# Opening of a one-core perceiver kernel in another order: keys and values of batch 0 ahead of norms and queries, in half transfers

## The chip, the cores and the metric

The kernel runs on one core of one Trainium2 chip. The metric is the time of one execution on the device in microseconds (us); lower is better. Runs of the kernel are compared on the same chip.

## What is computed (the reference, cut)

One layer of a perceiver on x of [16, 64, 512]: cross attention to a context of [16, 1601, 512], self attention with a low-rank addition (LoRA) to its queries and values, and a mixture of 20 experts of which each token takes two. Dropped below: reshapes and the constants.

```python
h = layernorm(x)                                     # 1024 rows of 512
q, k, v = h @ w_q.T, ctx @ w_k.T, ctx @ w_v.T        # 16 heads of 32
s = where(mask == 0, -1e9, q @ k.T / sqrt(32))       # mask [64, 1601], one for all batches
x = x + (softmax(s) @ v) @ w_o.T
x = x + self_attention(layernorm(x))                 # qkv with LoRA on q and v, projection
h = layernorm(x)
g = top2(softmax(gelu(h @ wg1 + bg1) @ wg2 + bg2))   # gates of 20 experts
x = x + sum_e g[:, e] * (h @ We[e] + be[e])
```

## The kernel before, in words

Every product of matrices is made in float32 by three matmuls (`mm3`, L196 to L198): an operand is split into a high part, rounded by ScalarE (ACT, `weight_hi`, `context`, `turn_x`: a copy into the rounded type), and a low part, the rest, subtracted by VectorE (DVE, `weight_lo`, `context`, `turn_x` with `rest`, L1081). So nothing is multiplied before ACT and then DVE have gone over it.

The 1601 keys are held as five chunks of 400, the last chunk first. A cross attention step n handles one batch: four products give its 400 keys for all heads (`k_part`, 12 matmuls of 400 columns each), three or four give tiles of 128 values (`v_part`, 12 matmuls of 512 columns), `s_part` gives scores in two halves, DVE takes their maxima under the mask (`maxima`), ACT the exponentials (`exps`), GpSimd (POOL) divides by the sums, DVE transposes (`turn`), 16 small transfers on the SP queue shuffle blocks between partitions (`shuffle`), and `pv_part` multiplies with the values one step later. Segment 0 has 16 steps, one for each batch. Further segments would follow only where the mask needs more than the first chunk: `cm`, `rows`, `fl`, `fr`, `frow` and `used` (L1103) work that out into `ids`, and `count` is read by every engine with `value_load` ahead of step 0.

Each engine runs its own instructions in order, and semaphores hold them back. `wait_ge(S["v_w"], 2)` means that the engine stops until the second weight's low part is done. The lists `uses` and `at` give each product one of three PSUM banks in turn.

The opening before: the SP queue loads constants, the first half of x, the mask twice (64 partitions each), then w_q, context 0, w_k, the second half of x, mask and exclusions, and w_v when w_q's buffer is free. DVE takes means and variances of x (`bn`), reduces the mask (L1292), scales by it (L1294 to L1301, L1118) and normalizes (`apply_x`). TensorE transposes x by fours (`turn_x`, `turn4`, L202), makes the first half of the queries, the rest of the transposes and the four key products of batch 0, and then the second half of the queries, where L198 ends at 60.6 us. Step 0 makes its scores and values after that.

Step 1 has extra work: after the last value evictions ACT rounds the output weight (`out_weight_hi`), DVE subtracts (`out_weight_lo`), and only then come `turn(1, 5)` to `turn(1, 7)`, which `shuffle(1)` and so `pv_part(1, ...)` of step 2 wait for.

At the experts: `tok` (L1585) names which rows of x each block of 128 tokens takes. POOL gathers them from memory (`load_tokens`, L1745), TensorE transposes (`turn_tokens`), and each `block_of` is one block. Between the table's product (L669) and the first transposes stand the expert biases: eight products of the gates with `be` (L659), which DVE adds to `x_sb` (L1590). When all blocks are done, rows are read back and added (L1632), and x is stored.

## Time and profile before

| | |
|---|---|
| median of 3 runs | 717.66 us (716.87 to 718.05) |
| profiled execution | 719.19 us, its span 717.4 us |
| TensorE (PE) busy in the span | 647.0 us (90%) |
| VectorE (DVE) busy | 444.9 us (62%) |
| ScalarE (ACT) busy | 324.6 us (45%) |
| GpSimd (POOL) busy | 286.7 us (40%) |
| data moved | 108.26 MB, mean 151 GB/s |

The span runs from the first to the last instruction that the profiler shows, and the execution's own time is 1.8 us longer. The busy shares are means over stages with different limits, so a change in the opening is read from the opening's rows.

### The profile page before, as it was taken

The page shows a single profiled execution, that of the slowest core. Times are in us where ns is not written, and L with a number is a line of the kernel's source. Part 1 is how long each engine was busy: PE and PEld are TensorE (multiplying, and loading weights), DVE is VectorE, ACT ScalarE, POOL GpSimd, SP SyncE. Part 2 cuts the span into 40 slices and gives each one's busy share as a digit, 9 for nine tenths or more (in the row PEclk, how much of TensorE's full clock was granted, in tenths as well). Part 3 has the DMA queues.
Part 4 walks back from the last instruction along what each step waited for, and adds up shares of the span by engine and source line. Part 5 has one row for each costly group of instructions (what it writes and reads, how often), then busy time and mean ns, then how long its engine had stood idle before and what let it go on. Part 6 is the DMA issues. An engine that isn't in the chain of part 4 may idle for free.

```text
span 717.4 us, 15912 instructions
## 1 busy us (share of the span) xinstructions
PE 647.0 (90%) x6305; PEld 529.0 (74%) x6305; DVE 444.9 (62%) x1002; ACT 324.6 (45%) x601; POOL 286.7 (40%) x259
## 2 busy tenths in 40 slices
PE   0899998999999999999999979999999748999960
PEld 0697887788888788888788868877787535888850
DVE  4855574755665645765654556445575467899956
ACT  1425453444434444544443335334365430899940
POOL 0003535544445534355534234321243315787420
PEclk9999999999999999999999999999999965999995
DMA  8511535566554566455556540210011933999819
GB/s 282 194 60 47 118 99 142 136 165 164 115 127 125 128 164 138 116 129 130 146 120 159 126 150 1 74 60 3 2 60 63 382 114 125 383 401 396 291 53 347
DMA packets 42695, 108.26 MB, mean 151 GB/s; under 512 B 8164, under 2 KB 8548, under 8 KB 41714
## 3 DMA queue, kind: packets, MB, share of 16 engines
q1 hardware_dynamic: 38210, 98.73, 46.6%
q0 software_dynamic: 4400, 8.41, 3.2%
q8 instruction: 53, 0.87, 0.5%
q14 instruction: 32, 0.26, 0.1%
HBM read 66.13 MB, written 13.44 MB: 111 GB/s over the span
## 4 chain that ended last, share of the span: by engine, by line
PE 79%; DVE 6%; PEld 3%; DMA 3%; issue 3%; ACT 2%; SPq 2%; POOL 0%; PEldq 0%; POOLq 0%; ACTq 0%; DVEq 0%
PE bank L196 23%; PE bank L198 21%; PE bank L197 21%; PE bank L337 4%; PE bank L321 3%; PE bank L202 3%; DMA raw<-in_wq 2%; SPq L1819 1%; DVE x_sb L1632 1%; PE bank L558 1%; PEld bank L198 1%; PE bank L545 1%; DMA wr<-scratch_ys 1%; PEld bank L196 1%; PE bank L659 1%
## 5 line engine op out<-in xcount | busy, mean ns | idle before, releaser
L1658 POOL TENSOR_SCALAR pp<-pp,rl 128x400 f32<-128x400 f32 x128 | 162.9, 1290 | 176.7 <-DVE rl L1163 176.7
L815 ACT ACTIVATE pp<-pp,acc 128x400 f32<-128x400 f32 x128 | 79.0, 619 | 68.0 <-DVE acc L1222 68.0
L1222 DVE CUSTOM_DVE_ANT_0 pp<-bank,cap 128x400 f32<-128x400 f32 x128 | 65.9, 571 | 61.1 <-PE bank L321 61.1
L1212 DVE STREAM_TRANSPOSE raw<-pp 128x512 f32<-128x512 f32 x128 | 83.9, 690 | 10.4 <-POOL pp L1658 5.8
L196 PE MATMUL bank<-chi,wk 128*128 128x400 f32 x256 | 90.1, 352 | 0.0
L197 PE MATMUL bank<-clo,wk 128*128 128x400 f32 x256 | 88.3, 345 | 0.0
L198 PE MATMUL bank<-chi,wk 128*128 128x400 f32 x256 | 88.3, 345 | 0.0
L196 PE MATMUL bank<-wv,chi 128*128 128x512 f32 x200 | 82.2, 411 | 0.0
L197 PE MATMUL bank<-wv,chi 128*128 128x512 f32 x200 | 78.7, 393 | 0.0
L198 PE MATMUL bank<-wv,clo 128*128 128x512 f32 x200 | 78.4, 392 | 0.0
L196 PE MATMUL bank<-wh,xu 128*128 128x512 f32 x148 | 63.4, 428 | 4.2 <-POOL xu L1684 3.5
L198 PE MATMUL bank<-wh,xu 128*128 128x512 f32 x148 | 59.8, 404 | 0.0
L197 PE MATMUL bank<-wh,xu 128*128 128x512 f32 x148 | 59.4, 402 | 0.0
L755 ACT ACTIVATE vv<-bank 128x512 f32<-128x512 f32 x50 | 28.1, 597 | 63.1 <-PE bank L198 32.7
L196 PEld LDWEIGHTS bank<-chi,wk 128*128 128x128 f32 x256 | 48.0, 188 | 10.0 <-issue 9.4
L1150 DVE COPY kk<-bank 128x400 f32<-128x400 f32 x32 | 18.3, 573 | 58.0 <-PE bank L198 58.0
L196 PEld LDWEIGHTS bank<-wv,chi 128*128 128x128 f32 x200 | 37.6, 188 | 18.7 <-issue 10.8
L197 PEld LDWEIGHTS bank<-clo,wk 128*128 128x128 f32 x256 | 48.1, 188 | 0.6
L198 PEld LDWEIGHTS bank<-chi,wk 128*128 128x128 f32 x256 | 48.0, 188 | 0.0
L198 PEld LDWEIGHTS bank<-wv,clo 128*128 128x128 f32 x200 | 37.7, 189 | 8.6
L755 ACT ACTIVATE kk<-bank 128x400 f32<-128x400 f32 x32 | 16.1, 504 | 61.1 <-PE bank L198 61.1
L197 PEld LDWEIGHTS bank<-wv,chi 128*128 128x128 f32 x200 | 37.8, 189 | 6.5
(241 smaller groups left out, 1296.8 us busy)
## 6 DMA issues: line engine op xcount, KB each, us to landing
pt<-raw SPq DMA_DIRECT2D x256, 128.0 KB, 2.4
wr<-in_We SPq DMA_DIRECT2D x13, 1024.0 KB, 11.1
craw<-in_ctx SPq DMA_DIRECT2D x16, 800.0 KB, 4.7
raw<-in_We SPq DMA_DIRECT2D x8, 1024.0 KB, 10.8
acc<-in_We SPq DMA_DIRECT2D x6, 1024.0 KB, 11.7
scratch_xn<-acc SPq DMA_DIRECT2D x16, 256.0 KB
wr<-scratch_ys SPq DMA_DIRECT2D x8, 512.0 KB, 7.1
x_sb<-in_x SPq DMA_DIRECT2D x2, 1024.0 KB, 9.0
```

The source lines that it names most:

```text
L196: pe.matmul(o, lhs[0], rhs[0], start=start, stop=False)
L197: pe.matmul(o, lhs[0], rhs[1], start=False, stop=False)
L198: return pe.matmul(o, lhs[1], rhs[0], start=False, stop=stop)
L202: last = pe.transpose(bank[0:n, k * 128:(k + 1) * 128], of(k), ident)
L321: last = pe.matmul(scores[64 * c:64 * c + 64, j, :], qc[r, 2 * half + c, 64 * b:64 * b + 64], kk[r, 2 * half + c, :], start=True, stop=True)
L337: last = pe.matmul(turned[32 * j:32 * j + 32, g, :].rearrange("p (a q) -> p a q", a=2), vv[:, (25 * (n // 8) + 3 * (n % 8) + i4) % 4, 128 ...
L755: return act.activation(dst, src, ACT.Copy)
L815: act.activation(frame(p8), frame(p8), ACT.Exp, bias=bias, scale=-1.0, accum_out=total).then_inc(S["a_exp"], 1)
L1150: dve.tensor_copy(kk[:, g, :], at("k", 4 * n + g)[:, 0:CW]).then_inc(S["v_k"], 1)
L1212: dve.transpose(square[:, :, :, 32 * p8:32 * p8 + 32].rearrange("p o i x -> p i o x"), pp[:, c:c + 512].rearrange("p (i o x) -> p i o x", ...
L1222: dve.tensor_tensor_reduce(out=frame(p8), in0=scores[:, p8 % 4, :], in1=cap[:, :], scale=-1.0, scalar=nm[:, b, p8:p8 + 1] if seg else 3e38 ...
L1658: pool.tensor_scalar(frame(p8), frame(p8), rl[:, n % 2, p8:p8 + 1], None, ALU.mult).then_inc(S["g_pn"], 1)
```

## The change

The first four transfers become halves of w_k and of context 0, each half of 128 partitions. Constants and `lora` follow, then w_v (when the first half of w_k has landed), half of x, the mask once over 128 partitions, w_q into free space of `acc` (when the second half of w_k has landed), and the other half of x. TensorE begins with the keys of batch 0 (`first_keys`): the first two of the four blocks of 128 inputs for all four groups, then the other two, in banks 4 to 7. Two value tiles follow, then the sums over masks (`any_masked`, a new product that brings together the two halves of the mask), the transposes of x and a third value tile, and four query products with the small products of the mask's bookkeeping and of LoRA between them. The first scores of step 0 come ahead of the second half of the queries. The low parts of w_v and w_q are split: DVE takes blocks 2 and 3, POOL blocks 0 and 1. `used` moves from the opening to step 1 behind `out_weight_lo`; the `value_load`s move to step 3. `pp` no longer shares its place with `xt`, so the maxima don't wait for the last query (`p_q` 8) any more; `shuffle(0)` does now, as `pt` still shares it. POOL's clearing of `pp` moves to the start. At the experts, biases 3 to 7 on TensorE and all eight additions on DVE move behind the last block. Some small tiles move into `zero`, `acc`, `raw` and `pp`, and the counts in waits change with the order.

```diff
+        pp = sb("pp", [128, 8 * D + PW], f32, lasting)
...
+        lora = acc[0:16, 0:D].rearrange("p (j n) -> p j n", j=4)
+        wq_in = acc[:, 2048:4096].rearrange("p (k n) -> p k n", k=4)
...
+        uses = [("v", 0), ("v", 1), ("x", 0), ("x", 1), ("v", 2), ("x", 2), ("x", 3)] + [("q", m) for m in range(4)]
+        uses += [("x", 4), ("x", 5), ("v", 3), ("x", 6), ("x", 7)] + [("q", 4 + m) for m in range(4)]
...
+            def any_masked():
+
+                pe.wait_ge(S["d_cst"], 16)
+                pe.wait_ge(S["v_cap"], 1)
+                for c in range(2):
+                    for h in range(2):
+                        last = pe.matmul(pb[3][64 * c:64 * c + 64, 0:NC_], ident[:, 64 * h:64 * h + 64], cm, start=(h == 0),
+                                         stop=(h == 1))
+                last.then_inc(S["p_ids"], 1)
...
+            def first_keys():
+
+                c = columns(0)
+                for half in range(2):
+                    pe.wait_ge(S["v_w"], half + 1)
+                    pe.wait_ge(S["v_ctx"], half + 1)
+                    for g in range(4):
+                        for k in (2 * half, 2 * half + 1):
+                            last = mm3(pe, at("k", g)[:, 0:CW], [w[:, k, g * 128:(g + 1) * 128] for w in wk],
+                                       [chi[:, k, c], clo[:, k, c]], k == 0, k == 3)
+                        if half:
+                            last.then_inc(S["p_k"], 1)
 
...
+            def opening():
+                first_keys()
+                v_part(0, 0)
+                v_part(0, 1)
+                any_masked()
+                turn_x(0)
+                turn_x(1)
+                v_part(0, 2)
+                turn_x(2)
+                turn_x(3)
+                queries(0)
+                turn_rows()
+                queries(1)
+                count_chunks()
+                queries(2)
+                lora_products()
+                queries(3)
+                s_part(0, 0)
+                turn_x(4)
+                turn_x(5)
+                v_part(0, 3)
+                turn_x(6)
+                turn_x(7)
+                s_part(0, 1)
+                for m in range(4, 8):
+                    queries(m)
...
-            biases(range(3, 8))
             turn_tokens(0)
...
+            biases(range(3, 8))
...
+            def first_half(half, w_arrived, ctx_arrived):
+                ks = slice(2 * half, 2 * half + 2)
+                act.wait_ge(*w_arrived)
+                copy(wk[0][:, ks], raw[:, 1, ks]).then_inc(S["a_w"], 1)
+                act.wait_ge(*ctx_arrived)
+                copy(chi[:, ks, columns(0)], craw[:, ks]).then_inc(S["a_ctx"], 1)
...
+            def opening():
+                first_half(0, (d_raw[0], 16), (S["d_ctx"], 16))
+                first_half(1, (d_raw[1], 16), (S["d_k1"], 16))
+                weight_hi(wv, raw[:, 0], (d_raw[0], 32))
+                k_part(0, 0)
+                k_part(0, 2)
+                value(0, 0)
+                weight_hi(wh[0], wq_in, (d_raw[1], 32))
+                value(0, 1)
+                turn_x(0)
+                turn_x(1)
+                value(0, 2)
+                turn_x(2)
+                turn_x(3)
+                queries(0)
+                context(1)
+                for m in range(1, 4):
+                    queries(m)
+                turn_x(4)
+                turn_x(5)
+                value(0, 3)
+                turn_x(6)
+                turn_x(7)
+                exps(0, 0, 0)
+                exps(0, 0, 1)
+                queries(4)
+                exps(0, 0, 2)
+                queries(5)
+                exps(0, 0, 3)
+                queries(6)
+                queries(7)
...
             def weight_lo(dst, src, n):
                 dve.wait_ge(S["a_w"], n)
-                rest(dst[1][:, :, :], src, dst[0][:, :, :]).then_inc(S["v_w"], 1)
+                rest(dst[1][:, 2:4, :], src[:, 2:4], dst[0][:, 2:4, :]).then_inc(S["v_w"], 1)
+
+            def first_half(half):
+                ks = slice(2 * half, 2 * half + 2)
+                dve.wait_ge(S["a_w"], half + 1)
+                rest(wk[1][:, ks], raw[:, 1, ks], wk[0][:, ks]).then_inc(S["v_w"], 1)
+                dve.wait_ge(S["a_ctx"], half + 1)
+                rest(clo[:, ks, columns(0)], craw[:, ks], chi[:, ks, columns(0)]).then_inc(S["v_ctx"], 1)
...
-                    if n == 0:
-                        dve.wait_ge(S["p_q"], 8)
...
+            def row_scales():
+
+                dve.wait_ge(S["p_ids"], 1)
+                own.on(dve.tensor_scalar(cm, pb[3][:, 0:NC_], 0.0, None, ALU.not_equal))
+                dve.wait_ge(own.sem, own.n)
+                own.on(dve.tensor_reduce(rows[:, 0:1], cm, AX.X, ALU.max))
+                dve.wait_ge(own.sem, own.n)
+                dve.tensor_scalar(rows[:, 1:2], rows[:, 0:1], SCALE, None, ALU.mult)
+                own.on(dve.tensor_scalar(rows[:, 2:3], rows[:, 0:1], -1.0, 1.0, ALU.mult, ALU.add))
+                dve.wait_ge(own.sem, own.n)
+                dve.tensor_scalar(fl[:, 1:NC_], cm[:, 1:NC_], rows[:, 2:3], None, ALU.max).then_inc(S["v_ids"], 1)
...
+            def opening():
+                dve.memset(fl[:, 0:1], 1.0)
+                first_half(0)
+                first_half(1)
+                weight_lo(wv, raw[:, 0], 3)
+                dve.wait_ge(d_x[0], 16)
+                for i in range(4):
+                    own.on(bn(i))
+                variance(0, 4)
+                dve.wait_ge(S["d_par"], 32)
+                dve.tensor_reduce(cm, mska, AX.X, ALU.max, apply_absolute_value=True).then_inc(S["v_cap"], 1)
+                k_part(0, 1)
+                k_part(0, 3)
+                row_scales()
+                scaled(0, 4)
+                apply_x(0)
+                apply_x(1)
+                weight_lo(wh[0], wq_in, 4)
+                turn_x(0)
+                apply_x(2)
+                turn_x(1)
+                apply_x(3)
+                turn_x(2)
+                turn_x(3)
+                dve.wait_ge(d_x[1], 16)
+                for i in range(4, 8):
+                    own.on(bn(i))
+                variance(4, 4)
+                dve.wait_ge(S["p_ids"], 2)
+                dve.tensor_reduce(fr, pb[3][0:NC_, 0:128], AX.X, ALU.max).then_inc(S["v_ids"], 1)
+                context(1)
+                dve.wait_ge(S["p_ids"], 3)
+                dve.tensor_copy(frow[:, 0:10], pb[3][0:1, 0:10]).then_inc(S["v_ids"], 1)
+                scaled(4, 4)
+                apply_x(4)
+                apply_x(5)
+                make_cap(0)
+                lora_folds()
+                turn_x(4)
+                apply_x(6)
+                turn_x(5)
+                apply_x(7)
+                maxima(0, 0, 0)
+                turn_x(6)
+                turn_x(7)
+                maxima(0, 0, 1)
+
...
                         out_weight_lo()
+                        used()
+                    elif n == 3:
+                        dve.wait_ge(S["v_ids"], 5)
+                        counted.append(dve.value_load(ids[0:1, 5:6], min_val=1, max_val=5))
...
-            biases(range(8))
...
+            biases(range(8))
...
+            pool.memset(one32[:, :], 1.0)
+            alone(pool.memset(pp[:, 0:8 * D].rearrange("p (t c) -> p t c", t=8)[:, :, 0:PW], 0.0))
+            alone(pool.memset(pp[:, 8 * D:8 * D + PW], 0.0))
+
+            def weight_lo(dst, src, n):
+                pool.wait_ge(S["a_w"], n)
+                pool.tensor_tensor(dst[1][:, 0:2, :], src[:, 0:2], dst[0][:, 0:2, :].bitcast(f32),
+                                   ALU.subtract).then_inc(S["g_w"], 1)
...
+            weight_lo(wv, raw[:, 0], 3)
             power(0, 4, (S["v_var"], 1), S["g_rstd"])
+            weight_lo(wh[0], wq_in, 4)
             power(4, 4, (S["v_var"], 2), S["g_rstd"])
-            pool.wait_ge(S["p_q"], 8)
-            alone(pool.memset(pp[:, 0:8 * D].rearrange("p (t c) -> p t c", t=8)[:, :, 0:PW], 0.0))
-            alone(pool.memset(pp[:, 8 * D:8 * D + PW], 0.0))
-            pool.wait_ge(S["v_ids"], 5)
...
+            sp.dma_start(raw[:, 1, 0:2], t["wk"][:, 0:2]).then_inc(d_raw[0], 16)
+            sp.dma_start(craw[:, 0:2, :], t["ctx"][0, 0][:, 0:2]).then_inc(S["d_ctx"], 16)
+            sp.dma_start(raw[:, 1, 2:4], t["wk"][:, 2:4]).then_inc(d_raw[1], 16)
+            sp.dma_start(craw[:, 2:4, :], t["ctx"][0, 0][:, 2:4]).then_inc(S["d_k1"], 16)
             sp.dma_start(cst[:, :], t["cst"]).then_inc(S["d_cst"], 16)
             sp.dma_start(lora[:, :, :], t["lora"]).then_inc(S["d_par"], 16)
-            xv = t["x"].rearrange("(i b) q d -> i (b q) d", b=2)
+            sp.wait_ge(d_raw[0], 16)
+            sp.dma_start(raw[:, 0], t["wv"]).then_inc(d_raw[0], 16)
             sp.dma_start(x_sb[:, 0:4, :], xv[0:4].rearrange("i p d -> p i d")).then_inc(d_x[0], 16)
-            for h in range(2):
-                sp.dma_start(mska[64 * h:64 * h + 64, :, :], t["rows"]).then_inc(S["d_cap"], 16)
-            sp.wait_ge(S["d_cst"], 16)
-            sp.dma_start(raw[:, 0], t["wq"]).then_inc(d_raw[0], 16)
-            sp.wait_ge(d_x[0], 16)
-            sp.dma_start(craw[:, :, :], t["ctx"][0, 0]).then_inc(S["d_ctx"], 16)
-            sp.wait_ge(S["d_cap"], 32)
-            sp.dma_start(raw[:, 1], t["wk"]).then_inc(d_raw[1], 16)
+            sp.dma_start(mska, t["rows"]).then_inc(S["d_par"], 16)
+            sp.wait_ge(d_raw[1], 16)
+            sp.dma_start(wq_in, t["wq"]).then_inc(d_raw[1], 16)
             sp.dma_start(x_sb[:, 4:8, :], xv[4:8].rearrange("i p d -> p i d")).then_inc(d_x[1], 16)
 
             def chunk_of(seg):
                 return sp.value_load(ids[0:1, seg:seg + 1], min_val=0, max_val=4)
...
                 if n:
                     sp.wait_ge(S["p_pv"], 2 * n)
+                else:
+                    sp.wait_ge(S["p_q"], 8)
```

## Rows read from the trace of the kernel before

**Rows 1.** Busy time by stage: PE, PEld, DVE, ACT, POOL, granted clock, DMA, GB/s

```profile
200.00:300.00 100.00, 100.00 (x1167) 83.62 (x1166) 59.34 (x148) 44.81 (x106) 46.13 (x37) 1.00 0.51 125
```

**Rows 2.** Chain of waits in the opening: start us, us, what

```profile
3.40 12.49 DMA raw<-in_wq
...
25.32 0.72 PE bank L196
26.05 0.43 PE bank L197
...
30.50 0.23 PE bank L196
...
38.90 0.87 PE bank L202 x8
```

**Rows 3.** Timeline of PE: the first key product of step 1

```profile
73.77 0.34 PE L196 MATMUL bank<-chi,wk 128*128 128x400 f32 x1
```

**Rows 4.** Busy time by half microseconds at the start (columns as rows 1)

```profile
3.50:4.00 0.50, 0.00 (x0) 0.00 (x0) 0.00 (x0) 0.00 (x0) 0.00 (x0) 1.00 0.50 78
...
4.50:5.00 0.50, 0.00 (x0) 0.00 (x0) 0.00 (x0) 0.00 (x0) 0.00 (x0) 1.00 1.07 418
```

**Rows 5.** Groups of instructions by shape: busy us, mean ns | idle before

```profile
L755 ACT ACTIVATE xt<-bank 128x512 fp32r<-128x512 f32 x8 | 4.6, 597 | 6.2 <-PE bank L202 6.2
...
L755 ACT ACTIVATE wh<-raw 128x2048 fp32r<-128x2048 f32 x1 | 1.9, 1912 | 13.9 <-DMA raw<-in_wq 13.9
...
L1222 DVE CUSTOM_DVE_ANT_0 pp<-bank,cap 128x400 f32<-128x400 f32 x16 | 8.2, 571 | 15.0 <-PE bank L321 15.0
...
L1081 DVE TENSOR_TENSOR xt<-bank,xt 128x512 fp32r<-128x512 f32 x8 | 5.4, 682 | 1.6 <-ACT xt L755 1.6
...
L1081 DVE TENSOR_TENSOR wh<-raw,wh 128x2048 fp32r<-128x2048 f32 x1 | 2.3, 2293 | 0.1
...
L1721 POOL TENSOR_TENSOR wh<-raw,wh 128x512 fp32r<-128x512 f32 x4 | 5.1, 1294 | 0.0
```

**Rows 6.** Timeline of DVE in the opening: mask scaling (first, last), `used` (first, last)

```profile
15.71 0.17 DVE L1294 TENSOR_SCALAR cm<-cm 128x5 f32<-128x5 f32 x1
...
16.50 0.23 DVE L1118 TENSOR_SCALAR rstd<-rstd,rows 128x4 f32<-128x4 f32 x1
...
29.72 0.14 DVE L1105 TENSOR_TENSOR frow<-frow,cst 1x5 f32<-1x5 f32 x1
...
30.95 0.13 DVE L1113 CAST ids<-frow 1x1 int32<-1x1 f32 x1
```

**Rows 7.** Chain of waits through steps 1 and 2

```profile
95.84 1.92 ACT wh L755
...
114.82 3.16 PE bank L337 x128
```

**Rows 8.** Waits of PE from 100 to 420 us: total, times, longest

```profile
PE bank L337 <- DMA pt<-raw: 2.5, 1, 2.5
```

**Rows 9.** Busy time around that wait (columns as rows 1)

```profile
115.50:116.00 0.50, 0.50 (x32) 0.50 (x25) 0.50 (x3) 0.00 (x0) 0.00 (x0) 0.50 0.97 397
...
118.50:119.00 0.50, 0.50 (x3) 0.44 (x2) 0.50 (x1) 0.50 (x2) 0.50 (x2) 0.68 0.00 0
```

**Rows 10.** Chain of waits ahead of the first expert block

```profile
597.89 5.52 PE bank L659 x10
603.41 1.06 PE bank L202 x4
...
605.96 0.76 PE bank L196
```

**Rows 11.** Tile xi (gathered tokens): gathers, and time to landing

```profile
L1745 POOL DMA_INDIRECT xi<-scratch_xn,tok x15: 997/1026/1541, 598.2 to 624.7; - x15
...
DMA to landing us min/median/max: 2.7/6.2/7.2
```

**Rows 12.** Timeline of DVE at the end: the first additions of expert rows

```profile
701.24 2.99 DVE L1632 SCALAR_TENSOR_TENSOR x_sb<-wr,gmg,x_sb 128x512 f32<-128x512 f32 x4 [8.75 <-DMA wr<-scratch_ys]
```

More of the change, by code:

```diff
@@ new lines, in turn_rows, with count_chunks, lora_products @@
+            def turn_rows():
+                pe.wait_ge(S["v_ids"], 1)
+                pe.transpose(pb[3][0:NC_, 0:128], fl[:, 0:NC_], ident).then_inc(S["p_ids"], 1)
+            def count_chunks():
+                pe.wait_ge(S["v_ids"], 2)
+                pe.matmul(pb[3][0:1, 0:10], fr, cst[0:NC_, 128:138], start=True, stop=True).then_inc(S["p_ids"], 1)
+            def lora_products():
+                pe.wait_ge(S["d_par"], 32)
+                pe.wait_ge(S["v_ids"], 3)
+                for j in range(2):
+                    last = pe.matmul(pb[3][:, j * 128:(j + 1) * 128], lora[:, 2 * j, :], lora[:, 2 * j + 1, :], start=True,
+                                     stop=True)
+                last.then_inc(S["p_ids"], 1)
@@ new lines, in turn_x, with queries @@
+                turn4(pe, at("x", i), lambda k: xn[:, i % 2, k * 128:(k + 1) * 128]).then_inc(S["p_xt"], 1)
+            def queries(m):
+                pe.wait_ge(S["v_w"], 4)
+                pe.wait_ge(S["g_w"], 2)
+                pe.wait_ge(S["v_xt"], m // 4 * 4 + 4)
+                for ready in freed("q", m):
+                    pe.wait_ge(*ready)
+                for k in range(4):
+                    last = mm3(pe, at("q", m)[:, :], [w[:, k, m % 4 * 128:(m % 4 + 1) * 128] for w in wh[0]],
+                               [v[:, k, :] for v in xt], k == 0, k == 3)
+                last.then_inc(S["p_q"], 1)
@@ L784, in k_part, with queries @@
                 copy(kk[:, g, :], at("k", 4 * n + g)[:, 0:CW]).then_inc(S["a_k"], 1)
[L786 to L789 removed]
+            def queries(m):
+                act.wait_ge(S["p_q"], m + 1)
+                copy(qc[:, m % 4, m // 4 * 512:(m // 4 + 1) * 512], at("q", m)[:, :]).then_inc(S["a_q"], 1)
             def early_hi(i):
@@ L820, in exps @@
                                    ACT.Exp).then_inc(S["a_cor"], 1)
+            def opening():
[29 more added lines that the diff above has]
+                queries(7)
             def cross(seg):
-                for n in range(16 * seg, 16 * seg + NB):
+                if not seg:
+                    opening()
+                for n in range(16 * seg or 1, 16 * seg + NB):
                     values = list(range(made(n), made(n + 1)))
@@ L1235, in cross @@
                     make_cap(seg)
+                else:
+                    opening()
                 for n in range(first, last + 1):
@@ L1242, in cross @@
                         k_part(n, 1)
-                    if n < last and n:
-                        context(n + 1)
-                    maxima(n, seg, 0)
-                    maxima(n, seg, 1)
-                    if n == 0:
-                        context(1)
+                        if n < last:
+                            context(n + 1)
+                        maxima(n, seg, 0)
+                        maxima(n, seg, 1)
                     share(n, 0, seg)
@@ L1816, in shuffle @@
                     sp.wait_ge(S["p_pv"], 2 * n)
+                else:
+                    sp.wait_ge(S["p_q"], 8)
                 for a in range(4):
@@ L2024 @@
         "mask": mask.reshape(64, NC, CW)[:, ::-1].transpose(1, 0, 2),
-        "rows": mask.reshape(64, NC, CW)[:, ::-1],
+        "rows": mask.reshape(64, NC, 2, CW // 2)[:, ::-1].transpose(2, 0, 1, 3).reshape(128, NC, CW // 2),
         "excl": excl,
```

249 lines of the change are left out of this document (71 added, 178 removed).

## The prediction

> **What bounds the kernel now.** First the busy time by stage: in the middle of the cross attention TensorE is busy for all of 100 us [rows 1], so there each microsecond by which step 1 begins earlier reaches the end, unless a later wait takes it back. Then the chain of waits through the opening: until 15.9 us it is the transfer of w_q, 12.5 us from its issue; then rounding, low parts, norms and transposes, and TensorE's first query product starts at 25.3 [rows 2]. From there TensorE has no gap until step 1 begins with its first key product at 73.77 [rows 3]. So the opening costs 25.3 us of an almost idle TensorE and 48.45 us of work. Third, the chain through steps 1 and 2: it leaves TensorE for ACT's output weight at 95.84 and returns with the values' product of step 1 at 114.8 [rows 7]; TensorE waited 2.5 us for that shuffle [rows 8]. Fourth, the chain ahead of the experts: biases, then transposes, then block 0 at 605.96 [rows 10].
>
> **Start of TensorE after.** First I estimate the landings. Up to 4.0 us little flows (78 GB/s in the half microsecond before it), and at 4.5 the rate is 418 GB/s [rows 4]; I put 0.3 MB at 4.0 and go on with 380 GB/s. The first half of w_k (0.52 MB) is there at 4.65, that of the context (0.41 MB) at 5.65, the second halves at 7.0 and 8.1. ACT takes 0.60 us for 512 columns and 1.91 for 2048, DVE 0.68 and 2.29, POOL 1.29 for 512 [rows 5]. Between these, 1024 columns are 1.04 on ACT and 1.22 on DVE, 800 columns 0.85 and 0.98. The halves pass: ACT w_k 4.7 to 5.7, DVE its low part to 7.0 while ACT rounds the context, DVE the context's low part to 7.9. TensorE starts at 8.0. Bounds: 7.0 if data come a microsecond sooner, 9.2 if the four pieces share the rate and the first land only at about 6.
>
> **Work from there to step 1.** The same products as before in another order: 48.45 us from 25.32 to 73.77, four transposes of which lie ahead of 25.3 now and come after the start: 1.75 (0.87 for eight single ones [rows 2] is 0.44 for each four). Small products (masks, rows, counts, LoRA) I put at 1.5, between nothing and the 2 us that several isolated ones would be. Cold matmuls: 0.43 us at first and 0.23 later in the old opening [rows 2], that is the level of 1.2 and then of 2.4 GHz for 512 columns, and the new opening pays a similar stretch on keys, so no difference.
>
> New gaps on TensorE, each a chain through other engines:
> - Before transpose 0: `any_masked` comes after value tile 1, so DVE's scaling can begin only then: 15.71 to 16.73 in the old order [rows 6], 1.0 us, then one norm of 512 columns (no more than the low part's 0.68) and hand-overs: 1.8.
> - Before query 0: the last two transposed tiles pass ACT (0.5 and 0.6) and DVE (0.68), less the 0.44 in which the last transposes run, with value tile 2's eviction ahead: 1.65.
> - Before the first scores: the last query's eviction on ACT, 0.60 and hand-overs: 0.7.
> - Before the second scores: value tile 3 and two x tiles on ACT (0.5, 0.5, 0.6), the last low part on DVE (0.68), two maxima (0.57 each), less 0.9 of transposes: 2.7.
>
> Together 6.85. Step 1 begins at 8.0 + 48.45 + 1.75 + 1.5 + 6.85 = 66.55.
>
> What hides the rest: w_v's low part on POOL is 2.6 us (twice 1.29) from about 14.0 and is wanted at 18.9, after 10.9 us of keys; alone on DVE it would be 2.3. w_q's on POOL runs 24.2 to 26.8 and is wanted at 32.9. Were that cover gone, query 0 would wait for POOL one for one. x's norms and the mask's reduction (half as many columns) end before 21 on DVE, some 4 us ahead of `any_masked`. `make_cap` and LoRA's folds lie under queries. POOL's clearing of `pp` moves to where POOL has nothing. On the SP queue, w_v waits for w_k's first half and w_q for its second; nothing in front of them is late for them, and w_q has until 22 on ACT. `shuffle(0)` now waits for `p_q` 8, that is until step 1 begins, where 16 steps of it and its landing fit under the 16 us of TensorE work before it is read. The reads of `count` fall on step 3 for all engines; I cost them at nothing, since TensorE's stood between queries and scores before, in the stretch without gaps, and at most at some tenths.
>
> **The clock.** After the 2.5 us wait [rows 8] the granted clock was 0.50 in 115.5 to 116 and came back at about 118.7 (0.68 in 118.5 to 119) [rows 9]; the values' product took 3.16 us there [rows 7]. About 3.5 us at half rate lose 1.75. Of the new gaps the one of 2.7 us is longer than that wait, so I charge it 1.75; those of 1.8 and 1.65 are shorter and I charge them nothing; the bounds are 0 and 1.75 for each. The Trainium skill, "TensorE: Matmul & The Clock Gate", section "HAM oscillation — how this bites in real kernels", says that a kernel whose TensorE waits between bursts falls back to the half clock and pays for the warm-up each time. The row on the 2.5 us wait agrees; for shorter gaps no row here shows it, and if the rule held for all three the sum would be 3.5 us more.
>
> So step 1 begins at 68.3 and the opening gains 73.77 - 68.3 = 5.5 us.
>
> **What is given back.** `used` stood at 29.72 to 31.08 [rows 6] in a stretch of DVE that nobody waited for. It now follows `out_weight_lo` in step 1, in front of the transposes 5 to 7 that `shuffle(1)` waits for, and that chain ends in the wait of 2.5 us [rows 7, 8]. That chain starts from TensorE's own third value tile, so it moves with TensorE and the wait doesn't shrink by the earlier start: it grows by 1.36. Loss 1.4; none if something else on that chain gave way.
>
> **Experts.** `tok` releases the gathers; the first is issued at 598.2 and a gather lands 2.7 us from issue at the least [rows 11], so at 601.0 or later. TensorE was with the biases until 603.41 [rows 10]. Without them: transposes 0 end at about 602.1 (1.06), ACT and DVE 0.60 and 0.68 [rows 5], while transposes 1 wait for the second gather, 1.3 us behind the first, and block 0 can start at 603.6 to 605.0. I take 604.2, a gain of 1.8 (1.0 to 2.3). The biases cost nothing at the end: DVE is free there for 8.75 us until 701.24 [rows 12], eight additions are some 5 us, and five products at the 5.52 us of now [rows 10] fit as well.
>
> **Sum.** -5.5 + 1.4 - 1.8 = -5.9. On the profiled execution, 719.19 to 713.3; its time is 1.5 above the median of 717.66, so for the median 711.8. No change within 0.2% (1.4 us) can be told from none.
>
> **Rivals.**
> 1. The forecast, 711.8: chance 0.50 (its own range 710.3 to 713.3).
> 2. The clock stays up through the 2.7 us gap. 1.75 less: 710.0. With an early start (7.0) and 2.3 at the experts, 708.5. Chance 0.22.
> 3. The clock falls at all three gaps: twice 1.75 more, 715.3. For it speaks the one wait that did so [rows 8, 9], against it that the gaps are a third shorter. Chance 0.15. This is the case in which the Trainium skill's section named above holds throughout.
> 4. The gain is lost further on: the wait at step 2 grows by more than `used` because `shuffle(0)` behind `p_q` 8 delays the queue, or the experts don't start earlier. It needs 4.5 us more; same as before, 716.5 to 718.5. Against it: TensorE is busy throughout behind step 2 [rows 1]. Chance 0.08.
> 5. Slower: the halves do not land first. All transfers are issued in a row and may share the engines, as w_q, issued at 3.4, needed 12.5 us [rows 2]. If w_k and the context landed like that, at about 13 to 15, TensorE would start at 15 to 16, and beyond 13.9 (8.0 + 5.9) the change loses: 719 to 720. Against it: the four are first in the queue, and w_q had 2 MB ahead of it. Chance 0.05.
>
> The range is 708.3 to 715.7: it leaves out rivals 4 and 5 and the far ends of 2 and 3. Faster 0.87, same 0.08, slower 0.05.
>
> **What would show it.** First key matmul at 8.0 (7.0 to 9.2); first key product of step 1 at 68.3; four gaps of 1.8, 1.65, 0.7 and 2.7 us on TensorE with a granted clock of 0.5 after the last alone; a wait of 3.9 us for the shuffle in step 2; block 0's start 1.8 us nearer to `tok`; additions of biases ended before the first expert rows. Wrong would be made most easily by the landing times and by the clock.

## The result, and the profile after

| | before | after |
|---|---|---|
| median, us | 718.62 (716.87 to 720.73, 6 executions) | 712.25 (710.65 to 713.12, 5 executions) |
| ratio, 95% interval | | 0.9907 [0.9882, 0.9932] |
| profiled execution, us | 719.19, span 717.4 | 712.70, span 710.8 |
| mean granted clock | 0.959 | 0.959 |

The forecast was 711.8 us, range 708.3 to 715.7, a gain of 5.9; the medians differ by 6.4. Two disturbed executions, one of 761 us here and one of 1073 us in the first experiment, are left out. The total is right, but three of its terms were not; so first the path through the changed kernel, stretch by stretch, on the two profiled executions.

The waits of TensorE in the first 200 us of the changed kernel (total, times, longest):

```profile
PE bank L193 <- DVE clo L1147: 8.3, 1, 8.3
PE bank L354 <- DVE acc L1297: 2.7, 1, 2.7
PE bank L199 <- DVE raw L1176: 2.6, 1, 2.6
PE bank L372 <- DMA pt<-raw: 2.4, 1, 2.4
PE bank L193 <- DVE xt L1147: 1.8, 1, 1.8
PE bank L354 <- issue: 1.8, 1, 1.8
PE bank L354 <- ACT qc L796: 0.8, 1, 0.8
```

TensorE starts at 8.3 (forecast 8.0); the four gaps of the opening are 2.6, 1.8, 0.8 and 2.7 (forecast 1.8, 1.65, 0.7, 2.7). The wait for the second shuffle is 2.4 us, as in [rows 8] and not 3.9 as forecast, but a new wait of 1.8 us stands at L354, before the first scores of step 2. The first key product of step 1, in the timeline of PE:

```profile
69.32 0.35 PE L193 MATMUL bank<-chi,wk 128*128 128x400 f32 x1
```

That is 4.45 us earlier than in [rows 3]; 5.5 were forecast. The values' products of steps 0, 1 and 2, in the chains of waits, of the changed kernel and then of the kernel before (where the middle one is in [rows 7]):

```profile
85.97 1.92 PE bank L372 x128
...
111.55 1.99 PE bank L372 x128
...
132.87 1.92 PE bank L372 x128
```

```profile
90.41 1.95 PE bank L337 x128
...
137.70 1.92 PE bank L337 x128
```

From the first to the third of them it is 46.90 us after and 47.29 before, so the stretch as a whole is not longer, though 1.4 us were forecast for `used`. Its two parts differ, though: from the first to the second it is 25.58 us for 24.41, 1.17 longer, and from the second to the third 21.32 for 22.88, since in the kernel before the clock fell at the second one ([rows 9]) and here it did not. The timeline of DVE in step 1 shows where it stands (first `used` instruction, then the key eviction behind it):

```profile
95.53 0.14 DVE L1180 TENSOR_TENSOR zero<-zero,cst 1x5 f32<-1x5 f32 x1
...
98.63 0.52 DVE L1225 COPY kk<-bank 128x400 f32<-128x400 f32 x1
```

The eviction ends at 99.15 and the scores start at 99.26. The 1.8 us wait, which the view puts down to "issue", is thus one for DVE.

The experts: the release of the row numbers, the start of block 0, and the end (the loads of result rows by SP, and DVE's last additions), and then the release and the end in the kernel before:

```profile
591.07 0.18 DVE tok L1672
...
598.47 0.76 PE bank L193
```

```profile
690.06 3.99 SPq L2050 DMA_DIRECT2D wr<-scratch_ys  x8
```

```profile
704.00 2.99 DVE L1718 SCALAR_TENSOR_TENSOR x_sb<-wr,gmg,x_sb 128x512 f32<-128x512 f32 x4 [0.61 <-DMA wr<-scratch_ys]
```

```profile
597.07 0.18 DVE tok L1585
```

```profile
697.97 4.47 SPq L1953 DMA_DIRECT2D wr<-scratch_ys  x8
```

```profile
704.90 8.79 DVE L1632 SCALAR_TENSOR_TENSOR x_sb<-wr,gmg,x_sb 128x512 f32<-128x512 f32 x12 [0.67 <-DMA wr<-scratch_ys]
```

From release to block 0 it is 7.40 us (8.89 before, 605.96 of [rows 10] less 597.07), from release to the first load of results 98.99 (100.90 before). From that load to the end of the last addition it is 16.93 us (15.72 before, 697.97 to 713.69).

The sum over the two executions: opening -4.45, steps 1 and 2 -0.39, from there to the release of the row numbers -1.17, experts -1.91, end +1.21, the rest +0.1; together -6.6, the difference of the spans. The opening gave less than forecast, the delay by `used` was made up by a fall of the clock that did not come, the experts gave what was forecast, and two terms that the sum did not have nearly cancel.

### The profile page after: what moved, and what is told of

Its sections match the earlier page's. It is cut to its first block, busy times and chain, and to the rows that moved or that the text cites. A ratio compares the mean times of both kernels' runs of the same rounds, so it can differ in the third digit from the quotient of the medians.

```text
span 710.8 us, 15960 instructions
## 1 busy us (share of the span) xinstructions
PE 642.0 (90%) x6313; PEld 525.4 (74%) x6313; DVE 442.3 (62%) x1004; ACT 325.2 (46%) x603; POOL 294.2 (41%) x261
## 4 chain that ended last, share of the span: by engine, by line
PE 80%; DVE 5%; issue 4%; PEld 3%; DMA 3%; ACT 2%; SPq 2%; POOL 0%; DVEq 0%; PEldq 0%; POOLq 0%; ACTq 0%
PE bank L193 23%; PE bank L195 21%; PE bank L194 21%; PE bank L372 4%; PE bank L354 4%; PE bank L199 3%; DMA wr<-scratch_ys 2%; SPq L1917 1%; PE bank L599 1%; PE bank L586 1%; PEld bank L195 1%; PEld bank L193 1%; PEld bank L194 1%; DMA craw<-in_ctx 1%; PE bank L615 1%
## 5 line engine op out<-in xcount | busy, mean ns | idle before, releaser
L193 PEld LDWEIGHTS bank<-wv,chi 128*128 128x128 f32 x200 | 38.0, 190 | 17.5 <-issue 9.4
L1147 DVE TENSOR_TENSOR xu<-bank,xu 128x512 fp32r<-128x512 f32 x44 | 29.8, 684 | 24.9 <-ACT xu L796 18.5
L796 ACT ACTIVATE kk<-bank 128x400 f32<-128x400 f32 x32 | 16.1, 504 | 60.9 <-PE bank L195 60.9
```

The lines of the kernel that those rows point to most:

```text
L193: pe.matmul(o, lhs[0], rhs[0], start=start, stop=False)
L796: return act.activation(dst, src, ACT.Copy)
L1147: return dve.tensor_tensor(dst, src, hi.bitcast(f32), ALU.subtract)
```

## The experiments

All medians stand beside the kernel before on the same chip: 718.61 us in experiments 1 to 4, 718.55 in 5's first execution and in 6 to 8, and on another chip 719.01 in the timed part of 5 and in 9 to 11. The changed kernel itself came again first, as a reference.

**1. The changed kernel, unaltered.**

> The changed kernel unaltered, once more, for its spread and as the reference of the other runs of this call. Theory: time 712 us (710.5 to 713.2), ratio to the kernel before 0.991; the idle times of TensorE in the opening come again as 2.6, 1.8, 0.8 and 2.7 us, because the order of the instructions sets them. Theory A for the clock: the order sets its falls too, so the granted clock is 0.5 at 29 to 31 us and 1.0 after the wait for the second shuffle, as in the first trace. Rival B: the falls depend on the moment, so the places change from one execution to the next with the same gaps, and the time with them by 1.2 to 1.6 us each.

713.12 us, ratio 0.9919 [0.9895, 0.9943]. The gaps are the same four: 2.6, 1.8, 0.8 and 2.7. The falls of the clock are not at the same places. The granted clock of the stretches 28 to 32, 56 to 60 and 100 to 105 us, first in the profiled execution of the result, then in this one (columns as rows 1, the third number from the right is the clock):

```profile
28.00:32.00 4.00, 4.00 (x13) 3.19 (x12) 2.81 (x5) 1.01 (x2) 0.00 (x0) 0.57 0.01 4
56.00:60.00 4.00, 2.85 (x25) 1.89 (x26) 3.12 (x14) 1.73 (x6) 2.82 (x3) 1.00 0.01 4
100.00:105.00 5.00, 5.00 (x32) 4.38 (x24) 3.94 (x12) 2.56 (x8) 1.62 (x2) 1.00 0.76 169
```

```profile
28.00:32.00 4.00, 4.00 (x26) 3.40 (x24) 3.05 (x5) 1.72 (x4) 0.00 (x0) 1.00 0.00 0
56.00:60.00 4.00, 4.00 (x24) 2.58 (x19) 2.85 (x10) 0.57 (x2) 4.00 (x4) 0.57 0.01 4
100.00:105.00 5.00, 5.00 (x31) 4.51 (x17) 4.15 (x12) 2.56 (x8) 1.41 (x2) 0.66 0.81 182
```

Behind the 2.6 us gap TensorE was slowed in one and not in the other; behind the 2.7 us gap it is the reverse; behind the 1.8 us wait of step 2 only the second one fell. Theory A falls, rival B holds for the places. One fall has the same price each time: one minus the clock, summed over the stretch, is 1.7 us (4 times 0.43, 5 times 0.34). So the falls in the column of the granted clock can be listed for every profiled execution of this study (summed in windows of 1 us, 3.4 where two follow each other; the slow first products of TensorE are not in that column):

| execution | falls in the opening, us | falls in steps 1 and 2 |
|---|---|---|
| before | none | 115-119 |
| changed, first | 28-32 | none |
| 1 | 56-60 | 100-105 |
| 2 | 54-59 | 99-103 |
| 3 | 26-34 (3.4) | 112-116 |
| 4 | 56-60 | 100-105 |
| 5, first | 27-31, 58-62 | 112-120 (3.4) |
| 5, timed | 56-60 | 100-105 |
| 6 | 29-33, 60-64 | 104-108 |
| 7 | 28-33 | none |
| 8 | 32-36, 55-60 | none |
| 9 | 31-36 | none |
| 10 | 54-59 | none |
| 11 | 56-61 | 111-115 |

The new opening has one or two falls in each of these, the old one had none.

**2. The mask's product ahead of value tile 1.**

```
                 v_part(0, 0)
+                any_masked()
                 v_part(0, 1)
-                any_masked()
```

> The mask's small product stands ahead of value tile 1 instead of behind it. Theory: the 2.6 us gap ahead of the first transposes is due to that place alone, so it goes (0 to 0.4 us left), DVE's small operation on the zero tile falls from 1.06 to 0.2 us since it no longer meets POOL's low part, and the fall of the clock behind the gap goes too: 2.4 us less in gaps and 1.2 to 1.7 less in slow products, step 1 begins 3.5 to 4 us earlier, time 708.3 to 709. Rival B: the clock falls at the gap of 2.7 us instead, then step 1 begins 2.4 us earlier and the time is 709.8. Rival C: the transposes wait for something else (the norms' reciprocal roots on POOL, the second half of x), the gap stays over 1.5 us and the time over 711.

710.76 us, ratio 0.9889 [0.9867, 0.9912], 2.4 us under experiment 1 by the medians (the intervals overlap). The 2.6 us gap is gone from the waits and DVE's operation took 0.23; one fall of the clock stayed, behind the 2.7 us gap. That is rival B; step 1's first scores came at 74.48 instead of 76.30, 1.8 of its 2.4 us. In this execution TensorE started 0.25 us earlier, but its slow first products lasted 6.3 us instead of 4.2, which at nearly half the rate costs about 0.9.

**3. `used` back in the opening.**

```
                 dve.tensor_copy(frow[:, 0:10], pb[3][0:1, 0:10]).then_inc(S["v_ids"], 1)
+                dve.wait_ge(S["v_ids"], 3)
+                used()
...
                         out_weight_lo()
-                        used()
```

> The seven small operations that work out the list of used chunks go back into the opening, behind the copy of the counts, instead of following the output weight's low part in step 1. Theory: they cost 1.3 us in step 1, by delaying DVE's key eviction, so that the first scores of step 2 wait 0.5 instead of 1.8 us, while the wait for the second shuffle stays at 2.4 to 2.5; nothing is lost in the opening; time 1.3 us less, 710.9. Rival B, as the prediction had it: they lengthen the wait for the second shuffle, which falls to 1.1 us, and the scores still wait 1.8; the same 1.3. Rival C: with 0.5 and 2.5 us of waits, as in the kernel before, the clock falls behind the second one and takes 1.6 us back: time 712.3 or a little more, no gain.

713.00 us, ratio 0.9916 [0.9895, 0.9936]: no gain. The scores of step 2 wait 0.5 us and the shuffle 2.7, and the clock falls behind the shuffle (values' product 3.59 us). Rival C holds in the trace; the medians alone, whose intervals are 2.9 and 3.4 us wide, could not tell 1.3 us from none. The values' products of steps 0, 1 and 2 here:

```profile
87.73 1.92 PE bank L372 x128
...
112.31 3.59 PE bank L372 x128
...
135.24 1.93 PE bank L372 x128
```

From the first to the third it is 47.51 us, against 46.90 and 46.67 with `used` in step 1 (the changed kernel's first execution and experiment 1). But from the first to the second it is 24.58, against 25.58 and 25.31: the delay by `used` is there, and what hides it is the place of the fall.

**4. The experts' biases back in their old place**, the last five products on TensorE as here, the additions on DVE in the same way.

```
             last.then_inc(S["p_tab"], 1)
+            biases(range(3, 8))
             turn_tokens(0)
...
-            biases(range(3, 8))
```

> The experts' biases go back to their old place ahead of the first transposes of the experts. Theory: the experts' first transposes of block 1 begin 2.0 us later against the release of the row numbers (11.8 us, 13.7 in the kernel before), and the tail behind the last block stays as it is in the changed kernel (16.9 us from the first load of results to the last addition), time 2.0 us more: 714.2. Rival B: the additions at the end cause the longer tail (15.7 us in the kernel before), so it shortens by 1.2 us with them gone and the net loss is 0.7: 713. Rival C: nothing at all, because the transfers of the experts' weights set the pace: 712.2.

715.97 us, ratio 0.9961 [0.9943, 0.9979], 2.9 above experiment 1. From release to the first load of results 101.4 us (99.3 in experiment 1, 100.90 before), so 2.1 of it is where the theory has it; from that load to the last addition 16.1. That tail is 15.7 and 16.1 with the biases early and 15.6 to 17.4 in the twelve profiled executions with the biases last; whether they have a part in it is left open.

**5. GpSimd's part of w_q later**, so that it does not meet DVE's scaling, in one execution and then timed.

```
+            pool.wait_ge(S["v_xn"], 2)
             weight_lo(wh[0], wq_in, 4)
```

> GpSimd's share of w_q's low part waits until DVE has written the first two norms, nothing else is altered. Theory: the 0.8 us by which the first gap was longer than forecast (2.6 for 1.8) come from DVE's small operation that took 1.06 us while GpSimd's low part ran; with the two apart it takes 0.2 and the gap is 1.8 us. GpSimd's part still ends before query 0 needs it, so that gap stays at 1.8. Rival: the operation is slow for a reason of its own (its operands, the clearing ahead of it), still takes 1.0, and the gap stays at 2.6.

> GpSimd's share of w_q's low part behind the first two norms once more, now timed, because its only execution so far took 718.75 us: the first gap was 1.8 us, as expected, but the records have falls of the clock that cost 10.2 us ahead of the experts' part, against 5.1 in the changed kernel. Theory: the falls come by chance and do not belong to this edit; the gap of 0.8 us less is all, median 711.5 to 713, some executions up to 718. Rival: the shorter gap brings the falls of the clock with it, and the median is 716 or more.

The first execution took 718.75 us, the five timed ones 713.28 (712.16 to 714.65), ratio 0.9933 [0.992, 0.9946]. In both the first gap is 1.8 us, as forecast for the changed kernel, and the operation takes 0.23. The theory on the gap holds, but it is worth no time that can be measured here. The first execution had four falls more up to 570 us than the changed kernel's first one (12.0 us against 5.1; the 10.2 of the expectation leaves one out), which is more than the 6.1 us between them; that such falls do not belong to the edit is read from the timed executions, none of which came near it. In both executions another operation of DVE met GpSimd's part instead. First the changed kernel, GpSimd then DVE, then the timed one:

```profile
14.38 3.40 POOL L1736 TENSOR_TENSOR wv<-raw,wv 128x1024 fp32r<-128x1024 f32 x1 [12.47 <-ACT wv L796]
...
24.02 2.35 POOL L1736 TENSOR_TENSOR wh<-acc,wh 128x1024 fp32r<-128x1024 f32 x1 [4.01 <-ACT wh L796]
```

```profile
14.26 1.23 DVE L1147 TENSOR_TENSOR wv<-raw,wv 128x1024 fp32r<-128x1024 f32 x1 [3.15 <-ACT wv L796]
...
25.34 1.06 DVE L1316 TENSOR_SCALAR zero<-zero 128x4 f32<-128x4 f32 x1
```

```profile
26.72 3.31 POOL L1736 TENSOR_TENSOR wh<-acc,wh 128x1024 fp32r<-128x1024 f32 x1 [6.25 <-DVE raw L1176]
```

```profile
28.29 2.03 DVE L1176 TENSOR_SCALAR raw<-x_sb,mv,rstd 128x512 f32<-128x512 f32 x1
```

In the changed kernel the operation at L1316 ends at 26.40, GpSimd at 26.37. In the timed one the norm, 0.54 us elsewhere, ends at 30.32, GpSimd at 30.03. And where DVE's low part runs first, GpSimd's takes 3.40 instead of 2.35: 15.49, the end of DVE's, plus 2.35 is 17.84, and it ends at 17.78. So of these operations the one that comes second waits until the first has ended. Other operations of DVE ran beside GpSimd's part unhindered (last section).

**6. Whole transfers of w_k and the context.**

```
-            sp.dma_start(raw[:, 1, 0:2], t["wk"][:, 0:2]).then_inc(d_raw[0], 16)
-            sp.dma_start(craw[:, 0:2, :], t["ctx"][0, 0][:, 0:2]).then_inc(S["d_ctx"], 16)
-            sp.dma_start(raw[:, 1, 2:4], t["wk"][:, 2:4]).then_inc(d_raw[1], 16)
-            sp.dma_start(craw[:, 2:4, :], t["ctx"][0, 0][:, 2:4]).then_inc(S["d_k1"], 16)
+            sp.dma_start(raw[:, 1], t["wk"]).then_inc(d_raw[0], 16)
+            sp.dma_start(craw[:, :, :], t["ctx"][0, 0]).then_inc(S["d_ctx"], 16)
```

> w_k and the context of batch 0 come in one transfer each instead of two halves; the rounding stays in halves. Theory: the start of TensorE follows from the landing of the context's first part, 6.2 us now; with 1.9 MB in two transfers of 1.05 and 0.82 MB, w_k lands at about 7, the context at about 9, and TensorE starts at 10.5 to 11 instead of 8.1; but the second halves are then rounded right away, so the keys of the second half no longer wait and some tenths come back: step 1 begins 2 us later, time 714.5 to 715. Rival: the pieces share the rate from the start, so the last byte of the first halves lands no earlier than the whole would, and TensorE starts at 8 to 9 with the time unchanged.

715.32 us, ratio 0.9955 [0.9939, 0.9972], 2.2 above experiment 1. TensorE starts at 9.6 instead of 8.1, not at 10.5: ACT's first pieces begin at 5.62 and 7.60, at 4.30 and 6.05 in experiment 1. So the start lies between theory and rival, and the time is near the theory's. The halves are worth 1.5 us at the start in this pair; with halves the start lies at 7.5 to 8.6 in twelve traces. With the edit w_v also waits for the whole of w_k, and w_q no longer waits for its second half. 1.7 more of this execution is a second fall of the clock.

**7. The output weight's low part later**, in halves at the ends of steps 2 and 4 instead of step 1.

```
                     if n == 1:
-                        out_weight_lo()
                         used()
+                    if n in (2, 4):
+                        out_weight_lo(n // 2 - 1)
```

> The output weight's low part, which DVE makes at the end of step 1, is made in two halves at the end of steps 2 and 4; the list of used chunks stays in step 1. Theory: DVE's wait for ACT's high part and the 2.3 us of the low part are what delays the turns, the key eviction and the second shuffle, so the 1.8 us wait for the scores and the 0.6 to 2.4 us wait for the shuffle in step 2 both go; a half of 1.2 us fits in the slack of a step (3.0 us, since step 1 was late by 3.0 us after a delay of 6.0). Pulling 3.3 to 4.2 us out of TensorE's idle time also takes away the fall of the clock there; time 708 to 709. Rival B: another transfer or engine ends last right behind, and waits of over 1.5 us appear in steps 2 to 5: 711 or more. Rival C: half of it shows, 710, because the fall of the clock only moves to a later place.

710.15 us, ratio 0.9884 [0.9865, 0.9903]. All waits of TensorE from the start to 200 us:

```profile
PE bank L193 <- DVE clo L1147: 8.6, 1, 8.6
PE bank L354 <- DVE acc L1298: 2.7, 1, 2.7
PE bank L199 <- DVE raw L1177: 2.6, 1, 2.6
PE bank L193 <- DVE xt L1147: 1.8, 1, 1.8
PE bank L354 <- ACT qc L796: 0.8, 1, 0.8
```

```profile
86.37 1.92 PE bank L372 x128
...
107.63 1.93 PE bank L372 x128
...
128.87 1.93 PE bank L372 x128
```

Both waits of step 2 are gone, and so is the fall of the clock there; from the first of the products to the third it is 42.50 us instead of 46.90. The profiled execution took 708.26 us as the theory says; the median, 3.0 us under experiment 1, shows about two thirds of it and lies where rival C has it. The five times lie at 708.3, 708.5 and three at 710.2; a fall of the clock more would be just that distance, but the three were not profiled, so whether it is rival C's later fall stays open.

**8. Experiments 2, 3 and 7 together.**

> The mask's small product ahead of value tile 1, the list of used chunks back in the opening, and the output weight's low part in halves at the end of steps 2 and 4, together. Theory: the gains add up where they are idle time of TensorE: 2.4 us from the first gap and 3.3 to 4.2 us from step 2, with one fall of the clock (1.7 us) left in the opening: time 706 to 707. Rival: the falls of the clock come back at other places and the sum is no better than the best single part, 708.5 or more.

705.66 us (703.70 to 706.28), ratio 0.9823 [0.9802, 0.9844]. The gains add up as the theory has it: 7.5 us under experiment 1, 2.4 from the gap and 4.4 from step 2 being 6.8. By the medians of experiments 2, 3 and 7 alone it would be 5.5; with intervals of some 3 us each the difference cannot be told from none. Two falls in the opening, none in steps 1 and 2.

**9. As 8, with the four maxima of the first scores ahead of the last two low parts of x.**

```
                 maxima(0, 0, 0)
+                maxima(0, 0, 1)
                 turn_x(6)
                 turn_x(7)
-                maxima(0, 0, 1)
```

> As the run with all three, and also DVE takes all four maxima of the first scores ahead of the last two low parts of x. Theory: the second scores wait for the last maximum alone, which now comes 1.2 us earlier and does not wait for ACT; the gap of 2.7 us falls to 0.8 to 1.0, query 4 then waits some 0.3 us for x, so 1.5 to 1.7 us are gained, and the fall of the clock that followed this gap in some executions is rarer: 703.5 to 704.2. Rival: the gap moves in full to query 4, which waits for the last low part as the scores did, and the time stays at 705.7.

704.50 us (703.14 to 705.15), ratio 0.9802 [0.9789, 0.9814], the best of this study. Its waits in the same stretch:

```profile
PE bank L193 <- DVE clo L1147: 7.5, 1, 7.5
PE bank L193 <- DVE xt L1147: 2.3, 2, 1.8
PE bank L354 <- DVE acc L1298: 0.9, 1, 0.9
PE bank L354 <- ACT qc L796: 0.8, 1, 0.8
```

The 2.7 us gap is 0.9, and query 4 waits 0.5: 1.3 us gained in the gaps, 1.2 in the medians (the intervals against the kernel before overlap).

**10. Experiments 2 and 7 without 3**, that is with `used` in step 1.

> The mask's product first and the output weight's low part later, but the list of used chunks stays in step 1. Theory: what it costs (1.3 us of DVE in step 1) only shows as long as step 1 has no slack; with the low part gone from there it fits, and the time is that of all three, 705.5 to 706. Rival: it costs its 1.3 us wherever step 1 ends in the shuffle: 707.

705.52 us (703.65 to 707.44), ratio 0.981 [0.9795, 0.9826], the same as 8. TensorE waits 0.3 us in step 2. With the low part gone from there, `used` costs nothing in step 1.

**11. Both low parts on DVE alone**, GpSimd's calls and TensorE's waits for them left away.

```
-                rest(dst[1][:, 2:4, :], src[:, 2:4], dst[0][:, 2:4, :]).then_inc(S["v_w"], 1)
+                rest(dst[1][:, :, :], src, dst[0][:, :, :]).then_inc(S["v_w"], 1)
```

> The changed kernel with both low parts whole on DVE, nothing on GpSimd. Theory: GpSimd's share is worth nothing, since DVE stands idle ahead of the mask's product (3.8 us) and query 0 waits for x and not for w_q; without it DVE's small operation takes 0.2 us, the first gap is 1.8 us and the time 0.8 us less or the same: 711.5 to 712.5. Rival B: the low part of w_q, 2.3 us on DVE instead of 1.2, delays the low parts of x, query 0 waits about 1.1 us longer: 713.5. Rival C: the low part of w_v comes after TensorE wants it, value tile 0 waits: over 714.

713.39 us (710.11 to 716.34), ratio 0.9918 [0.9894, 0.9942], the same as experiment 1. The operation takes 0.23 us, the first gap is 1.8, query 0 waits 1.5 and not longer. GpSimd's share is worth nothing that this measures.

This trace also settles what `used` costs. It has `used` in step 1 behind the low part, and the clock falls behind the shuffle, as in the kernel before and in experiment 3:

```profile
85.59 1.92 PE bank L370 x128
...
111.48 3.59 PE bank L370 x128
...
134.39 1.51 PE bank L370 x97
```

From the first to the third it is 48.80 us, against 47.29 and 47.51 without `used` there and the fall at the same place: 1.3 to 1.5 us.

## Why the prediction came out right

**Start of TensorE: right**, 8.3 for 8.0 (7.0 to 9.2), and the four pieces do land first. The path was another: the forecast had DVE held by w_k's low part until 7.0; it ended at 6.55, and what set the start was the context's first half, landed at 6.24 instead of 5.65, and the two passes over it. Halves against whole transfers are worth 1.5 us there (experiment 6).

**Work to step 1: right in sum.** 51.7 us were forecast for products old and new; 69.32 less the start, the gaps (7.9) and one fall (1.7) leaves 51.4. Some of that is luck: the slow first products were put as long as before, but lasted 3.3 us in this execution and 4.9 before, which is worth about 0.7, and in the other traces of the new order they lasted 3.3 to 6.5.

**Gaps: one term mis-sized.** "1.8" before transpose 0 measured 2.6. It was worked out from the old order of the small operations, in which GpSimd was idle; the new order put GpSimd's low part beside them, and one of them waited for its end (experiment 5: 1.8 with the two apart). The other three are within 0.15. The gaps together are 7.9 for 6.85, the start is 0.3 late, the work 0.3 less: step 1 was forecast at 68.3 and began at 69.3. The Trainium skill, "SBUF — State Buffer", section "Who interferes with whom", says that VectorE and GpSimd share a pair of ports, and that where a VectorE instruction of certain kinds needs it, the one that issues first holds it for the whole instruction and the other waits. The ends in experiment 5 agree with it.

**The clock: right in size, not in place.** 1.75 was charged for one fall, and a fall costs 1.7. It was charged to the 2.7 us gap because that is the longest. In the first profiled execution the clock fell behind the 2.6 us gap, in experiment 1 behind the 2.7 us one, with the same gaps in both; in experiment 5's first execution and in 8 and 9 it fell behind gaps of 1.8. The length of a single gap does not decide. What the forecast had as three cases with one answer each (one fall, none, three) is a spread from execution to execution, one or two falls here. Nor did the count grow over the whole path: up to 570 us the first profiled execution has three falls and so has the kernel before, which has none in the opening and one in step 2. Of what the prediction cites from the Trainium skill, the traces bear out that a fall is paid for where no wait follows it, and not that each of these gaps brings one; the waits in that section's example are 3 to 5 us, longer than any gap here.

**What is given back: the step that failed.** "it grows by 1.36. Loss 1.4". The wait for the shuffle did not grow, and the stretch did not get longer. The delay itself came: from the values' product of step 0 to that of step 1 it is 25.3 to 26.4 us in the eight traces that have `used` behind the low part in step 1, and 24.4 and 24.6 in the two that have the low part there without it, about 1.4 in the middle. But `used` stands ahead of the key eviction too, so 1.3 us of it show before the scores (1.8 for 0.5), where TensorE and the shuffle's chain are late by the same amount and the shuffle's wait stays as it was. What the forecast put at nothing without a reason is the clock behind that wait: it kept the fall of the kernel before. In the first profiled execution the clock fell at neither wait, which gave back 1.6 us, more than the 1.2 that `used` cost there. In experiment 1 it falls behind the earlier wait, so that slow products fill time in which TensorE would wait for the shuffle anyway (0.6 us are left of that wait); without `used` it falls behind the shuffle and its 1.7 us come on top. In experiment 11 and in 5's first execution it falls behind the shuffle with `used` in place, and then the stretch is longer, 48.80 and 50.40 us. So a fall that stays away, or lies ahead of a wait, hides the loss; whether `used` itself moves the fall, and what makes it come at the one place or the other, is open.

**Experts: right.** 1.8 (1.0 to 2.3) forecast, 1.5 at block 0 and 1.9 at the first load of results, 2.1 in experiment 4. The 0.4 between the first two is the clock, which the forecast did not have: block 0's first products ran at half rate for 4.6 us before and 3.7 after.

**What the sum did not have.** -1.17 between step 2 and the release of the row numbers: before, the clock fell at 432 to 437 behind a wait of 1.5 us for the output weights' low part, after at 420 to 425, and that wait was absent; experiment 2 has the wait again. +1.21 at the end: the loads of result rows landed later against their issue, within what other executions show. Neither belongs to the change as far as these runs tell. So of the 0.45 us by which forecast and median differ nothing can be concluded: an opening 1.05 us worse than forecast and steps 1 and 2, 1.8 us better than forecast because the fall of the clock there stayed away, cancel, and that is luck.

**Rivals.** 2 and 3 both take the clock as fixed by the gaps, which experiment 1 refutes. 4, the gain lost further on, did not come: steps 1 and 2 take 0.4 us less. 5 is refuted by the start at 8.3. After the change 4.2 us of waits stand in step 2 (3.0 before), and experiment 7 shows their cause: DVE waits for ACT's output weight (3.7 us) and then makes its low part (2.3), ahead of the turns and of the key eviction.

## What to carry to other kernels

When an operation is moved, look for what is queued behind it on every path: the one that waits first is not always the one that waited before. A wait that stands at both ends of a stretch is removed by moving the long operation that delays both, not the short one beside it: 2.3 us of low part out of step 1, with the 3.7 us wait ahead of it, gave 4.4 us in the traces, 1.3 us of small operations gave nothing that the medians show. A change whose sum comes out can hide a loss behind a fall of the clock that moved; part the stretch at the fall, and compare executions in which it fell at the same place. And a forecast of the clock should be a number of falls times their price, with a spread, not a fall tied to a gap.

## What the runs showed of the hardware

A DVE operation on four columns took 1.06 us instead of 0.23, and a norm 2.03 and 1.82 instead of 0.54, each until GpSimd's subtraction of two blocks had ended; started behind DVE's subtraction, GpSimd's took 3.28 to 3.43 instead of 2.35. Not all of DVE's operations were held up: beside GpSimd's subtraction its statistics of x took 0.66 to 0.69 us, its small operations on one and five columns 0.14 to 0.17, and the low part of x, which reads its input from PSUM, 0.69, as in experiment 11 without it.

A fall of TensorE's clock from 2.4 to 1.2 GHz took 1.70 or 1.71 us off the granted clock ahead of the experts in every one of these traces, or twice that, and came at other places in two executions of one kernel with the same waits. The slow stretch at TensorE's first products is not in the column of the granted clock, which shows 1.00 there; it is seen in the products alone, one of 400 columns after the other 0.33 us apart from 8.8 to 11.1 us and 0.18 apart from 11.4 on. It ended 3.3 to 6.5 us after TensorE's start in the thirteen traces of the new order, a spread of some 1.4 us of time between executions.
